# Attention normalised in 32x32 blocks: VectorE turns, GpSimd multiplies, ScalarE copies

## The reference

```python
qkv = x @ Wqkv + bqkv                                  # 16 heads of 16
scores = einsum('bhid,bhjd->bhij', q, k) / 4 + alibi_causal_bias
out = softmax(scores) @ v                              # back to (b, s, 256)
x = layernorm(x + out @ Wo + bo)
h = silu(x @ tern(W_up).T) * (x @ tern(W_gate).T)      # 1024 wide, ternary weights
x = layernorm(x + h @ tern(W_down).T)
```

## Time and profile before

| what | value |
|---|---|
| times of three runs | 620.04, 624.6, 696.24 us |
| median | 624.6 us |
| span of the profiled execution | 619.3 us |
| the profiled execution's own time | not listed; the run nearest to its span is the one of 620.04 us |
| PE busy | 583.6 us (94%) |
| DVE busy | 494.4 us (80%) |
| ACT busy, POOL busy | 318.8 us (51%), 299.0 us (48%) |
| mean granted TensorE clock | 0.983 |

### The profile page before, as it was taken

The page is one execution under the profiler, slowest core; times in us unless marked ns, Lnnn a source line. Parts: engine busy times, 40 slices in busy tenths (PEclk is TensorE's granted clock), DMA queues, the critical chain, the costliest instruction groups (busy, mean ns, idle before and its releaser), DMA issues.

```text
span 619.3 us, 12888 instructions
## 1 busy us (share of the span) xinstructions
PE 583.6 (94%) x4012; PEld 342.5 (55%) x4012; DVE 494.4 (80%) x1258; ACT 318.8 (51%) x593; POOL 299.0 (48%) x504
## 2 busy tenths in 40 slices
PE   5789888999999999999999999999999999999995
PEld 3344354664656555674556646575556646446674
DVE  5388968996799868989599877989599877993766
ACT  2129713459247644477246653476345753576262
POOL 1306695346275535465174543654264452654234
PEclk9789998999999999999999999999999999999998
DMA  6965715005462073502653064601644054600101
GB/s 158 289 175 206 211 51 161 23 29 163 122 172 66 3 229 115 166 1 83 161 166 100 1 199 123 160 28 52 186 144 127 1 166 105 206 2 3 35 1 35
DMA packets 47724, 68.49 MB, mean 111 GB/s; under 512 B 4857, under 2 KB 43641, under 8 KB 44793
## 3 DMA queue, kind: packets, MB, share of 16 engines
q1 hardware_dynamic: 47691, 68.08, 37.5%
HBM read 38.44 MB, written 29.36 MB: 109 GB/s over the span
## 4 chain that ended last, share of the span: by engine, by line
PE 78%; DVE 5%; ACT 5%; POOL 5%; issue 4%; DMA 2%; SPq 0%; POOLq 0%; DVEq 0%
PE ring L698 17%; PE max_bank L613 10%; PE acc L647 9%; PE ring L635 9%; PE ring L590 8%; PE acc L715 7%; PE ring L597 4%; ACT probs L772 4%; PE ring L671 4%; PE max_bank L618 2%; PE ring L655 2%; POOL probs L1042 2%; PE ring L684 1%; POOL tern_down L1085 1%; PE max_bank L715 1%
## 5 line engine op out<-in xcount | busy, mean ns | idle before, releaser
L772 ACT ACTIVATE probs<-ring 128x512 f32<-128x512 f32 x320 | 170.7, 606 | 45.6 <-PE ring L635 44.0
L1042 POOL TENSOR_SCALAR_AFFINE_SELECT probs<-probs 128x256 f32<-128x256 f32 (+1 forms) x320 | 120.5, 401 | 130.1 <-ACT probs L772 129.4
L896 DVE CUSTOM_DVE_ANT_0 max_bank<-max_bank,causal_wide 128x384 f32<-128x384 f32 (+1 forms) x256 | 157.2, 637 | 15.3 <-PE max_bank L613 12.2
L613 PE MATMUL max_bank<-k_stack,q_stack 112*128 112x384 bf16 (+3 forms) x512 | 123.4, 304 | 5.9 <-DVE neg_max L896 2.8
L1078 POOL TENSOR_TENSOR hidden_lo<-hidden,hidden_hi 128x512 f16<-128x512 f32 (+1 forms) x72 | 75.1, 1050 | 63.6 <-ACT hidden_hi L803 63.3
L635 PE MATMUL ring<-q_stack,k_stack 114*128 114x512 bf16 (+3 forms) x512 | 103.7, 300 | 1.6 <-DVE attn L921 0.5
L791 ACT ACTIVATE gating<-ring,tanh_scale 128x512 f32<-128x512 f32 (+1 forms) x72 | 45.8, 639 | 74.0 <-PE ring L698 74.0
L647 PE MATMUL acc<-probs,v_ones 128*32 128x512 f32 (+3 forms) x1024 | 79.9, 437 | 2.8 <-POOL probs L1042 2.8
L613 PEld LDWEIGHTS max_bank<-k_stack,q_stack 112*128 112x128 bf16 x512 | 46.5, 98 | 54.0 <-DVE neg_max L896 15.3
L900 DVE TENSOR_REDUCE neg_max<-max_bank 128x2 f32<-128x512 f32 (+1 forms) x96 | 63.7, 686 | 10.4 <-PE max_bank L618 8.7
L635 PEld LDWEIGHTS ring<-q_stack,k_stack 114*128 114x128 bf16 x512 | 44.5, 97 | 49.4 <-issue 17.0
(11 more groups left out here) (107 smaller groups left out, 866.0 us busy)
## 6 DMA issues: line engine op xcount, KB each, us to landing
q_stack<-qk_scratch SPq DMA_DIRECT2D x15, 768.0 KB, 6.1
k_stack<-k_slots SPq DMA_DIRECT2D x15, 768.0 KB, 7.8
qk_scratch<-qk_parts SPq DMA_DIRECT2D x16, 384.0 KB, 3.0
k_slots<-qk_parts SPq DMA_DIRECT2D x16, 384.0 KB, 2.6
xin<-x_dram SPq DMA_DIRECT2D x8, 512.0 KB, 3.5
...
```

The source lines that it names most:

```text
L613: mm = pe.matmul(max_bank[k][:, width * i:width * (i + 1)], q_stack[0:MAX_ROW, 4 * g + h, P * tile:P * (tile + 1)], k_stack[0:MAX_ROW, 4 * ...
L772: rg.drained(act.activation(probs[:, g % 2, n, :], rg.bank(step)[:, :], ACT.Exp), step)
L896: dve.tensor_tensor_reduce(scores, scores, causal_wide[:, SEQ - width:SEQ], -1.0, LOWEST_START, ALU.add, ALU.min, neg_max[:, g, first_col: ...
L1042: return pool.affine_select(out=v, in_=v, compare_op=ALU.is_ge, fill=0.0, base=0, pattern=([[0, blocks]] if blocks > 1 else []) + [[1, P]] ...
```

## The change

Four things:

1. The PE transposes `nt.g` and `at.f` are gone, with their six ring banks. `turn.g` (DVE) turns `acc` in 32x32 blocks straight into `pv_t`; `nt_out.g` is now the reciprocal on DVE and the product on POOL, into `mixed`; `at.f` is a second block-wise turn on DVE, from `mixed` to `attn_t`. This leaves the rows of `attn_t` in another order, so `wo` is loaded in that order, by eight DMAs in FIRST (`load_wo.1`); the old order is loaded into `attn_t` for the bias in PRE.
2. ACT no longer copies `acc` (g 0, 1) nor `at.f`, and DVE no longer copies `acc` (g 2, 3).
3. ACT copies both halves of `x_t` (`tx.1` leaves DVE).
4. `v` has two steps of two tiles instead of four of one, each with one ACT copy.

```diff
-RING_STEPS = ("tx", "qk", "v", "at", "x1t", "up", "gate", "mt", "nt", "exp", "bias_fold", "wsum")
+RING_STEPS = ("tx", "qk", "v", "x1t", "up", "gate", "mt", "exp", "bias_fold", "wsum")
...
 FIRST_ORDER = """
...
+    qk_out.1 turn.1 split.1 wsum exp.3.4 exp.3.5 exp.3.6 exp.3.7 nt_out.1 at.0 exp.3.8 pv.2.0 exp.3.9 pv.2.1
+    ternary.0 ternary.2.0 pv.2.2 pv.2.3 turn.2 ternary.2.1 pv.3.0 part_write.0.2 pv.3.1 pv.3.2 part_write.1.0
+    ternary.1 part_write.1.1 part_write.1.2 nt_out.2 pv.3.3 ternary.2.2 turn.3 nt_out.3 wo.0.0 wo.1.0 at.1 wo.0.1
+    stack_read.0 wo.1.1
...
 SECOND_ORDER = """
...
+    pv.1.3 ffn_stats.0 exp.3.0 exp.3.1 ffn_stats.1 exp.3.2 exp.3.3 pv.2.0 exp.3.4 exp.3.5 nt_out.0 exp.3.6 exp.3.7
+    exp.3.8 pv.2.1 pv.2.2 pv.2.3 exp.3.9 turn.1 ln2 turn.2 nt_out.1 at.0 pv.3.0 load_res pv.3.1 pv.3.2
+    part_write.1.2 nt_out.2 pv.3.3 turn.3 wo.0.0 nt_out.3 at.1 stack_read.0 store wo.1.0 wo.0.1 wo.1.1
...
 LOOP_ORDER = """
...
+    take.3.9 pv.1.0 take.3.10 pv.1.1 ffn_stats.1 exp.2.6 mt.3 exp.2.7 mt_out.3 qk.0 exp.2.8 turn.0 ln2 exp.2.9
+    qk_out.0 pv.1.2 part_write.0.0 pv.1.3 nt_out.0 exp.3.0 exp.3.1 store split.0 exp.3.2 qk.1 exp.3.3 part_write.0.1
+    exp.3.4 turn.1 exp.3.5 qk_out.1 exp.3.6 exp.3.7 exp.3.8 nt_out.1 at.0 exp.3.9 pv.2.0 split.1 pv.2.1 pv.2.2
+    pv.2.3 pv.3.0 turn.2 part_write.1.0 part_write.0.2 pv.3.1 pv.3.2 part_write.1.1 nt_out.2 pv.3.3 turn.3 nt_out.3
+    part_write.1.2 wo.0.0 at.1 wo.1.0 wo.0.1 wo.1.1 stack_read.0
...
 SEVENTH_ORDER = """
...
+    exp.3.6 exp.3.7 exp.3.8 down.7 exp.3.9 pv.2.0 nt_out.1 at.0 ffn_sum.0 pv.2.1 pv.2.2 ffn_stats.0 ffn_sum.1 pv.2.3
+    pv.3.0 ffn_stats.1 pv.3.1 pv.3.2 pv.3.3 turn.2 nt_out.2 turn.3 nt_out.3 at.1 ln2 wo.0.0 wo.0.1 store wo.1.0
+    wo.1.1
...
@@ SyncE
+                            rows = w_o.rearrange("(f e h d) n -> f h e d n", f=FT, e=2, d=DH)
+                            for f in range(FT):
+                                for h in range(4):
+                                    sp.dma_start(wo[32 * h:32 * (h + 1), f, :], rows[f, h]).then_inc(wo_in, 16)
@@ TensorE
-                    elif kind == "nt":
...
-                    elif kind == "at":
...
                     elif kind == "wo":
...
-                            rg.wait_drained(pe, ("at", f))
-                            pe.wait_ge(weights_in[1], 32)
+                            at_least(pe, attn_turned, FT, b, f + 1)
+                            pe.wait_ge(wo_in, 16 * 4 * FT)
@@ VectorE
-                    elif kind == "pv" and step[1] >= 2 and step[2] == TT - 1:
+                    elif kind == "turn":
                         g = step[1]
+                        if not (first and g == 0):
+                            at_least(dve, mixed_done, QUADS, b, g - 1)
                         at_least(dve, acc_filled[g % 2], 3, b, g // 2 + 1 - acc_skipped(name))
-                        dve.tensor_copy(pv_t[:, g % 2, :], acc[g % 2][:, :]).then_inc(acc_drained[g % 2], 1)
+                        dve.transpose(pv_t[:, g % 2, :], acc[g % 2][:, :]).then_inc(acc_drained[g % 2], 1)
...
                         dve.reciprocal(inv_sum[:, g % 2, :, :], heads[:, :, DH:DH + 1]).then_inc(inverted, 1)
...
+                    elif kind == "at":
+                        f = step[1]
+                        at_least(dve, mixed_done, QUADS, b, 2 * f + 2)
+                        dve.transpose(attn_t[:, f, :], mixed[:, f, :]).then_inc(attn_turned, 1)
@@ GpSimd
+                    elif kind == "nt_out":
+                        g = step[1]
+                        heads = pv_t[:, g % 2, :].rearrange("p (s c) -> p s c", c=32)
+                        at_least(pool, inverted, QUADS, b, g + 1)
+                        if g % 2 == 0 and not (first and g == 0):
+                            at_least(pool, attn_turned, FT, b, g // 2 - 1)
+                        pool.tensor_tensor(
+                            mixed[:, g // 2, :].rearrange("p (s c) -> p s c", c=32)[:, :, DH * (g % 2):DH * (g % 2 + 1)],
+                            heads[:, :, 0:DH], inv_sum[:, g % 2, :, :].broadcast_to([P, TT * 4, DH]),
+                            ALU.mult).then_inc(mixed_done, 1)
```

More of the change, by code:

```diff
@@ L134 @@
[L134 to L138, removed]
@@ L139 @@
-    exp.3.8 pv.2.0 exp.3.9 pv.2.1 ternary.0 ternary.2.0 pv.2.2 pv.2.3 nt.2 ternary.2.1 pv.3.0 part_write.0.2 pv.3.1
-    pv.3.2 part_write.1.0 ternary.1 part_write.1.1 part_write.1.2 nt_out.2 pv.3.3 at.0 ternary.2.2 nt.3 nt_out.3
-    wo.0.0 wo.1.0 at.1 wo.0.1 stack_read.0 wo.1.1
+    qk.2 qk.3 part_write.2.0 split.2 max.0.0 max.0.1 max.0.2 max.0.3 max.0.4 max.0.5 max.0.6 part_write.3.0 take.0.0
+    max.0.7 max.0.8 take.0.1 take.0.2 max.0.9 take.0.3 take.0.4 v.0 max.0.10 max.1.0 take.0.5 take.0.6 split.3
@@ L154 @@
[L154 to L156 removed]
+    max.0.0 max.0.1 qk.2 take.0.0 max.0.2 max.0.3 take.0.1 take.0.2 max.0.4 max.0.5 v.0 take.0.3 max.0.6 take.0.4
+    take.0.5 take.0.6 max.0.7 qk.3 take.0.7 ln1 max.0.8 v_out.0 max.0.9 load_next x1t.0 x1t.1 take.0.8 split.2
@@ new lines @@
+    hidden_hi.3 up.6 up.7 swiglu.4 mt_out.0 max.2.0 swish.5 max.2.1 take.1.9 exp.0.0 take.1.10 gate.6 swiglu.5
+    hidden_hi.4 max.2.2 max.2.3 take.2.0 take.2.1 swish.6 down.2 v.1 hidden_hi.5 take.2.2 max.2.4 take.2.3 swish.7
+    max.2.5 v_out.1 take.2.4 down.3 exp.0.1 max.2.6 tx.0 swiglu.6 hidden_hi.6 take.2.5 take.2.6 tx.1 exp.0.2 max.2.7
+    exp.0.3 take.2.7 max.2.8 gate.7 mt.1 max.2.9 take.2.8 exp.0.4 swiglu.7 qk.0 take.2.9 mt_out.1 exp.0.5 qk_out.0
+    down.4 qk.1 exp.0.6 hidden_hi.7 max.2.10 split.0 max.3.0 down.5 exp.0.7 take.2.10 max.3.1 take.3.0
@@ L185 @@
-    split.0 exp.3.2 qk.1 exp.3.3 part_write.0.1 exp.3.4 nt.1 exp.3.5 qk_out.1 exp.3.6 exp.3.7 exp.3.8 nt_out.1
-    exp.3.9 pv.2.0 split.1 pv.2.1 pv.2.2 pv.2.3 pv.3.0 nt.2 part_write.1.0 part_write.0.2 pv.3.1 pv.3.2
-    part_write.1.1 nt_out.2 pv.3.3 at.0 nt.3 nt_out.3 part_write.1.2 wo.0.0 at.1 wo.1.0 wo.0.1 wo.1.1 stack_read.0
+    qk.2 max.0.0 max.0.1 take.0.0 qk.3 take.0.1 max.0.2 ln1 x1t.0 max.0.3 x1t.1 max.0.4 v.0 take.0.2 load_res
+    take.0.3 max.0.5 part_write.3.0 max.0.6 max.0.7 x1_lo.0 take.0.4 take.0.5 part_write.2.0 x1_lo.1 v_out.0 split.2
@@ L208 @@
-    ffn_stats.0 ffn_sum.1 pv.2.3 pv.3.0 ffn_stats.1 pv.3.1 pv.3.2 pv.3.3 nt.2 nt_out.2 nt.3 at.0 nt_out.3 at.1 ln2
-    wo.0.0 wo.0.1 store wo.1.0 wo.1.1
+    qk.2 max.0.0 max.0.1 max.0.2 take.0.0 take.0.1 max.0.3 ln1 load_res take.0.2 x1t.0 v.0 split.2 max.0.4 x1t.1
+    max.0.5 v_out.0 take.0.3 x1_lo.0 qk.3 take.0.4 part_write.3.0 max.0.6 take.0.5 max.0.7 x1_lo.1 max.0.8 take.0.6
+    up.0 take.0.7 part_write.2.0 take.0.8 max.0.9 take.0.9 gate.0 swish.0 max.0.10 take.0.10 part_write.2.1 max.1.0
@@ new lines @@
+    up.1 mt.0 take.1.0 gate.1 max.1.1 up.2 v.1 max.1.2 part_write.2.2 swiglu.0 max.1.3 split.3 hidden_hi.0
+    part_write.3.1 mt_out.0 swish.1 up.3 max.1.4 v_out.1 take.1.1 part_write.3.2 swiglu.1 swish.2 take.1.2 exp.0.0
+    gate.2 hidden_hi.1 take.1.3 max.1.5 take.1.4 swish.3 max.1.6 gate.3 up.4 max.1.7 swiglu.2 take.1.5 stack_read.1
+    hidden_hi.2 exp.0.1 take.1.6 max.1.8 swiglu.3 up.5 take.1.7 gate.4 max.1.9 exp.0.2 max.1.10 exp.0.3 hidden_hi.3
+    up.6 exp.0.4 take.1.8 exp.0.5 max.2.0 exp.0.6 swish.4 swish.5 swiglu.4 take.1.9 max.2.1 take.1.10 exp.0.7
```

172 lines of the change are left out of this document (66 added, 106 removed).

## The result

The changed kernel takes 667.75 us (median of four runs, 666.22 to 672.61), the kernel before 623.27 (median of 620.04, 621.94, 624.6 and 696.24). The last of these is a slow execution, and the ratio, 1.074 with the interval 1.068 to 1.080, leaves it out. The direction was forecast, the size was not: 45.2 us between the two spans in place of 27.5, and the range ended at 658. The profiled execution has a span of 664.5 us, with a mean granted clock of 0.957.

A forecast was written before the change was run, and what follows sets the result against it. PE was taken to bound the kernel, 94% busy and setting LOOP's pace; 11.8 + 7.0 + 8.5 - 0.9 + 1.1 = 27.5 us on the 619.3 span gave a forecast of 647 us, range 624 to 658.

The forecast's parts named there:

- The wait in front of `split.1`: LOOP: `at.0` waits for POOL's product, delaying `split.1`, the stack read and `max.0.0`; +2.35 us per iteration, +11.8 in five.
- step 2: LOOP timing: product to 295.8, `at.0` to 296.5, so `split.1`, begun at 292.50 before, is 4.0 us late.
- The clock: LOOP: PE's idling brings a drop to half clock, costing 0 to 1.6 us, taken 1.4 per iteration, 7.0 in five.
- -2.2 us an iteration: LOOP: gain from fewer PE transposes and a shorter tail relay, provided nothing is queued behind a new wait.
- the `v` products are as many as before: LOOP: the count of `v` products stays the same; the two ACT copies instead of four lie in ACT's idle time.
- The faster rival: PE work rules: `at.0` delays `split.1` too little to matter, LOOP gains 2.2 us per iteration; 613 or 604 us; chance 0.12.
- FIRST: Products queue among POOL's 17.0 us of ternary work, so SECOND starts at 94 to 100, not 86.05; +8.5 us (7 to 13).
- SECOND: Product of quad 2 queues behind `res` additions, relay gains about 0.5; with PE and ACT relieved, -0.9 us (-2 to +1).
- SEVENTH: `at.0` before `ffn_sum.0` waits for the product, and DVE's backlog delays the last residual sum; +1.1 us (-1 to +3).
- The durations: New operations: `turn` 0.69 and `at` 0.65 us on DVE, bounds 0.42 to 1.4; product on POOL 0.73, bound 1.2.
- slow-turns rival: DVE turns take 1.4 us, adding 7 us in LOOP and some 2 in FIRST and SEVENTH; about 656 us; chance 0.08.
- the signs named: Profile after: DVE waits some 3 us, `k_stack` read about 4 later, PE idle in LOOP and FIRST, period 73 or 74.5.

The follow-up runs named there:

- e1: Changed kernel with `at.0` moved behind `split.1` in the LOOP text: 643.72 us, ratio 1.038 to the kernel before.
- e3: Changed kernel with the four products of a batch on DVE, right behind their reciprocals, orders unchanged: 640.12 us, ratio 1.032 to the kernel before.
- e12: Changed kernel with 12 matmuls that nothing reads on PE ahead of the wait for the stacks, in LOOP and SEVENTH: 665.47 us, ratio 1.074.
- e9: Changed kernel with FIRST reordered: DVE's ternary work before `at.0`, POOL's begun when three of DVE's four operations are done: 662.55 us, ratio 1.068.
- e8: e1 with `qk_out.1` ahead of `turn.1`, the product behind the last mask, and SEVENTH's `at.0` behind `ffn_stats.1`: 638.62 us, ratio 1.027.

## Why the prediction was right in kind and wrong in size

- **The wait in front of `split.1`** (+2.35 an iteration, +11.8): right in place, mechanism and price. 2.74 was measured where the steps say 2.79; e1 and e3 take the wait away in two different ways, and of PE's 3.0 us for the stack e1 leaves at most 0.1 and e3 0.5 to 0.8. DVE was free for `split.1` at 311.46 and began it at 315.44, 4.0 us later, as step 2 has it.
- **The clock** (+1.4 an iteration, +7.0): the term was wrong in its cause. The half clock came, in three of five iterations, and keeping it full (e12, and e9 by itself) gave at most 0.5. What fills its place in front of `qk.1` is 2.1 us an iteration of something else. From `max.0.0` to `qk.1` it is 53.5 us before and 54.6 to 54.8 in e1, where the clock is full, `ln1` takes 1.37 and no stack is waited for: 1.2 us, and the waits that stand there are the 0.4 to 0.7 for `ln1` and the 0.71 for `neg_max`. The first iteration of the changed kernel has 54.65 too; the others 55.5 to 56.5, with `ln1` stretched to 2.6 to 3.6 beside POOL's additions. So about 0.9 goes with that stretch: the stack's wait pushed `ln1` into the additions, and without it (e1) they don't meet. LOOP is 24.4 us instead of 18.8.
- **-2.2 us an iteration "if nothing is queued behind a new wait"**: this failed, though the sum hid it. With the wait gone LOOP stands at 71.0, and at 70.55 with two more steps moved, against 70.63. PE's work fell by 2.8 us in e1, and its waits rose by 2.9. PE 99% busy was read as PE's pace deciding whatever the change put in front of it; `turn.1` ahead of `qk_out.1` (0.98), the product ahead of the last mask (0.78, where 0.36 stood) and the relay (0.72, where 0.32 stood) were not in the sum. Nor was item 4: "the `v` products are as many as before" puts it at nothing, and 1.1 to 1.4 us of e1's waits stand where `v` was moved. The faster rival failed for this reason, beside its FIRST.
- **FIRST** (+8.5, 7 to 13; measured +14.9): the step that failed most. It has POOL's ternary operations at their old durations and everything else waiting for POOL. In fact DVE's ternary work began 4.3 us later (75.20 for 70.88; 1.97 of it are `at.0`'s wait and turn, 1.62 `turn.1`'s wait for `acc`), POOL's 1.3 us earlier (75.50 for 76.84), and two of DVE's four operations took 5.7 and 5.8 us for about 2.4 and 1.4. Before, three of them were over and the fourth had begun, at 76.63, when POOL's began. The row of 7.47 us in rows 7 was itself such a meeting: in e9, with nothing of DVE's ternary work beside it, that operation takes 5.44. e3 shows that the products' place in POOL's queue isn't needed for the loss, e9 the pace without the overlap. 10.5 of the 14.9 lie behind the first ternary operation. The 4.3 ahead of it rest on one profile of the kernel before; six profiles with the changed FIRST text have that operation at 75.20 to 79.21.
- **SECOND** (-0.9; measured -2.4): the sign is right partly by luck. Before, SECOND's `ln1` took 3.42 us beside POOL's `split.2` and PE waited 1.6 us for it; after the change it takes 1.38, and no step had that. **SEVENTH** (+1.1; measured +8.2): missed. `at.0` in front of `ffn_sum.0` waits 9.44 us; e8 prices it at 4.2 by moving it. Of the other 4.0, 2.3 are gone in e1 with LOOP's wait for the stack, which the step had left out, and in e3 all 8.2 are gone.
- **The durations**: turns 0.693 and 0.711 (taken 0.69 and 0.65), product 0.654 (taken 0.73). All within their bounds, so the slow-turns rival is out.

The terms missed by +5.6 (LOOP), +6.4 (FIRST), -1.5 and +7.1, in all 17.6 of the 45.2 us. The range was too narrow because its unknowns were bounded one by one, and no term stood for one delay that makes the next. Of the signs named, DVE's wait for the product (3.35 us), the `k_stack` read 4.1 us later within the iteration, PE's wait for it and FIRST's wait for POOL's third operation all came; the period, 75.5, came out above both of the two named.
